# Quantising w1 and w2 with the contraction on the partitions: maxima from blocks on the rows, scales through memory, no transposes

## The reference, cut to what matters

```python
def nf4_quant_dequant(w):                      # blocks of 64 along each row of w
    flat = w.reshape(-1, 64)
    absmax = jnp.max(jnp.abs(flat), axis=1, keepdims=True)
    normalized = flat / jnp.where(absmax == 0, 1.0, absmax)
    idx = jnp.searchsorted((NF4_CODE[:-1] + NF4_CODE[1:]) * 0.5, normalized)
    return (NF4_CODE[idx] * absmax).reshape(shape)

dq1, dq2, dq3 = (nf4_quant_dequant(w) for w in (w1, w2, w3))   # (1376,512), (1376,512), (512,1376)
h = silu(x @ dq1.T) * (x @ dq2.T)
return layernorm(x + h @ dq3.T)
```

## Time and profile before

| | |
|---|---|
| median of 3 runs (lowest, highest) | 429.75 us (429.55, 430.0) |
| time of the profiled execution | 429.79 us |
| its span, first to last instruction | 428.0 us |
| granted TensorE clock, mean over the span | 0.994 |
| busy: PE, PEld, DVE | 418.1, 343.0, 309.3 us |
| busy: ACT, POOL | 260.4, 274.5 us |
| DMA | 26.51 MB in 10876 packets |

### The profile page before, as it was taken

The page is one execution under the profiler, slowest core; times in us unless marked ns, Lnnn a source line. Parts: engine busy times, 40 slices in busy tenths (PEclk is TensorE's granted clock), DMA queues, the critical chain, the costliest instruction groups (busy, mean ns, idle before and its releaser), DMA issues.

```text
span 428.0 us, 5616 instructions
## 1 busy us (share of the span) xinstructions
PE 418.1 (98%) x1908; PEld 343.0 (80%) x1908; DVE 309.3 (72%) x390; ACT 260.4 (61%) x345; POOL 274.5 (64%) x219
## 2 busy tenths in 40 slices
PE   8999999999999999999999999999999999999992
PEld 7888888888878887888878888888888878888881
DVE  4539979788779979955568999998998884215025
ACT  5576766585586565548746786788667763332612
POOL 0079898798695699238953667699866853344330
PEclk9999999999999999999999999999999999999997
DMA  7994110100114432020060000000000000000202
GB/s 269 398 356 149 51 38 25 27 25 26 25 49 130 137 123 74 0 100 1 0 265 1 2 0 2 0 2 1 1 2 0 2 0 0 2 2 2 98 0 99
DMA packets 10876, 26.51 MB, mean 62 GB/s; under 512 B 1472, under 2 KB 1728, under 8 KB 10336
## 3 DMA queue, kind: packets, MB, share of 16 engines
q1 hardware_dynamic: 10848, 26.16, 17.9%
HBM read 24.06 MB, written 2.10 MB: 61 GB/s over the span
## 4 chain that ended last, share of the span: by engine, by line
PE 84%; POOL 8%; issue 5%; DVE 2%; ACT 0%; POOLq 0%
PE PS L1145 27%; PE PS L1147 27%; PE PS L1146 26%; POOL l_lo L1100 4%; PE PS L1259 2%; PE PS L1277 1%; POOL level L1070 1%; PE PS L1270 1%; POOL w_lo L1089 1%; POOL x_lo L1089 1%; DVE stats L876 0%; POOL Q L1061 0%; DVE R L871 0%; PE PS L1245 0%; ACT R L644 0%
## 5 line engine op out<-in xcount | busy, mean ns | idle before, releaser
L1070 POOL TENSOR_SCALAR level<-side 128x1024 f32<-128x1024 int8 (+2 forms) x119 | 130.0, 1093 | 25.9 <-ACT side L558 15.8
L801 DVE TENSOR_TENSOR PS<-PS,level 128x1024 f32<-128x1024 f32 (+2 forms) x102 | 121.8, 1194 | 24.1 <-POOL level L1070 19.8
L1145 PE MATMUL PS<-x_hi,w_hi 128*128 128x512 f32 (+1 forms) x352 | 138.4, 393 | 0.0
L1147 PE MATMUL PS<-x_hi,w_lo 128*128 128x512 f32 (+1 forms) x352 | 137.2, 390 | 0.0
L1146 PE MATMUL PS<-x_lo,w_hi 128*128 128x512 f32 (+1 forms) x352 | 137.1, 389 | 0.0
L558 ACT ACTIVATE side<-Q 128x1024 int8<-128x1024 f32 (+1 forms) x77 | 77.6, 1050 | 13.3 <-DVE PS L797 7.2
L1100 POOL TENSOR_TENSOR l_lo<-h,l_hi 128x512 fp32r<-128x512 f32 (+1 forms) x42 | 56.3, 1348 | 42.3 <-ACT l_hi L558 41.6
L1147 PEld LDWEIGHTS PS<-x_hi,w_lo 128*128 128x128 f32 (+1 forms) x352 | 65.2, 185 | 14.7
L1145 PEld LDWEIGHTS PS<-x_hi,w_hi 128*128 128x128 f32 (+1 forms) x352 | 65.3, 185 | 14.4 <-issue 0.3
L1146 PEld LDWEIGHTS PS<-x_lo,w_hi 128*128 128x128 f32 (+1 forms) x352 | 65.3, 185 | 14.3
L1145 PE MATMUL PS<-x_hi,l_hi 128*128 128x512 f32 x144 | 56.8, 395 | 0.6 <-POOL l_lo L1100 0.6
(11 more groups left out here) (77 smaller groups left out, 509.0 us busy)
## 6 DMA issues: line engine op xcount, KB each, us to landing
Q<-w SPq DMA_DIRECT2D x20, 256.0 KB, 9.8
raw<-w_in SPq DMA_DIRECT2D x9, 512.0 KB, 9.1
raw<-w_out SPq DMA_DIRECT2D x14, 256.0 KB, 2.6
raw<-w SPq DMA_DIRECT2D x2, 1376.0 KB, 7.8
R<-xN SPq DMA_DIRECT2D x2, 1024.0 KB, 5.2
out<-R SPq DMA_DIRECT2D x8, 256.0 KB, 2.1
raw<-w_fuse SPq DMA_DIRECT2D x7, 256.0 KB, 2.7
h<-xT SPq DMA_DIRECT2D x3, 512.0 KB, 6.6
```

What stands on the lines that cost most here:

```text
L801: v.tensor_tensor(total, total, level_of(s), ALU.add).then_inc(s_add, 1)
L1070: g.tensor_scalar(level_of(s), side_of(s), LIMITS[k][1], LIMITS[k][0], ALU.min, ALU.max).then_inc(s_level, 1)
L1145: t_.matmul(dst, a_hi, b_hi, start=start, stop=False)
L1147: return t_.matmul(dst, a_lo, b_hi, start=False, stop=stop)
```

## The change

For units 1 to 10 (`turned`) the maxima and the codes are computed on two layouts of the same numbers. The host passes w1 and w2 in two forms: `w12`, where a unit's blocks of 64 lie so that the 128 partitions get the blocks in order (`natural`, read only for the maxima), and `w12T`, with the contraction on the partitions, in the layout that the products read. DVE takes maxima and reciprocals from the first; SP writes both to a scratch tensor `scr` in memory (`to_memory`) and reads them back broadcast, each over the 64 partitions of its block, to full width (`from_memory`: four DMAs for a unit, in contiguous runs of up to 128 numbers). POOL then multiplies the turned unit by the full-width reciprocals (`rcp_wide`), DVE the sum by the full-width maxima (`amax_wide`). The result needs no transpose: `split_nf4` and `lo_nf4` read Q. Unit 0 is done as before.

These moves stand in SP's list between the loads of the weights, in the order `MOVES`, as many at each place as a new list `SHARE["sync"]` says. Their buffers: the last two units of Q while those are not in use, `raw`'s columns 4096 to 5119 (so `raw` has four slots instead of five for the weights, and splits are done three jobs ahead instead of four), and for unit 10 `raw` and two slots of `l_hi`. Scales are made 12 steps ahead (7 for unit 10). w3's first half is loaded when unit 10 is normalised, its second when unit 9 is dequantised. All SHARE lists are new, and two splits on ACT stand ahead of the last `scale_and_shift` of layer 1.

```diff
-SCALES_AHEAD, NORMALISE_AHEAD = 5, 3
+TURNED_AHEAD, LAST_AHEAD, SCALES_AHEAD, NORMALISE_AHEAD = 12, 7, 5, 3
...
+MOVES = [(1, "scales"), (2, "natural")]
+for u_ in range(1, C2):
+    MOVES.append((u_, "rcp"))
+    if u_ + 1 < C2:
+        MOVES.append((u_ + 1, "turned"))
+        if u_ + 2 == C2:
+            MOVES.append((u_ + 1, "natural"))
+        MOVES.append((u_ + 1, "scales"))
+        if u_ + 2 < C2 - 1:
+            MOVES.append((u_ + 2, "natural"))
+    MOVES.append((u_, "amax"))
+MOVES += [(C2 - 1, "w3 first"), (C2 - 1, "w3 second")]
...
-RAW_SLOTS = 5
-W_AHEAD = 4
+RAW_SLOTS = 4
+W_AHEAD = 3
...
 SHARE = {
+    "sync": [
+        0, 2, 1, 1, 5, 2, 3, 2, 5, 3, 4, 3, 2, 3, 0, 0, 0, 0, 0, 0, 0, 0, 0, 2, 0, 0, 0, 2, 0, 3, 0, 7, 0],
...
+            def to_memory(u):
+                n = unit_blocks(u)
+                sp.wait_ge(s_prep, scaled(u))
+                if u >= 3:
+
+                    sp.wait_ge(s_at, 32 * (u - 2))
+                for k, t in enumerate((amax, rcp)):
+                    sp.dma_start(scr[u % 2, k, 0:P * n].rearrange("(p n) -> p n", n=n), t[:, u % t.shape[1], 0:n]).then_inc(s_scr, 16)
+
+            def from_memory(u, k, to, done):
+                p = chunk_rows(u)
+                sp.wait_ge(s_scr, 32 * u)
+                blocks = scr[u % 2, k, 0:2 * DC * 2 * p].rearrange("(q r f) -> r q f", r=2, f=p)
+                for r in range(2):
+                    sp.dma_start(to[r * BLOCK:(r + 1) * BLOCK, 0:2 * DC * p].rearrange("p (q f) -> p q f", f=p),
+                                 blocks[r:r + 1].broadcast_to([BLOCK, 2 * DC, p])).then_inc(done, 16)
...
+            def rcp_back(u):
+                if u >= 2:
+                    sp.wait_ge(s_nrm, normalised(u - 1))
+                if u == C2 - 1:
+                    wait_split(sp, len(JOBS) - 1)
+                    wait_split(sp, VECTOR_LOW[-1])
+                from_memory(u, 1, rcp_wide(u), s_rc)
+
+            def amax_back(u):
+                if u >= 2:
+                    sp.wait_ge(s_dq, quantised(u - 1))
+                if u == C2 - 1:
+
+                    sp.wait_ge(s_tile, TT)
+                from_memory(u, 0, amax_wide(u), s_at)
+
+            def load_natural(u):
+
+                sp.wait_ge(s_prep, scaled(u - 1))
+                if u == C2 - 1:
+                    wait_split(sp, len(JOBS) - 1)
+                    wait_split(sp, VECTOR_LOW[-1])
+                load_unit(u)
...
             for j in range(RAW_SLOTS, len(JOBS)):
                 if j == JOB[1, AGAIN[0]]:
+                    beside()
                     load_residual(0)
+                beside()
                 load_job(j)
+            beside()
             load_residual(1)
-
-            wait_split(sp, len(JOBS) - 1)
-            wait_split(sp, VECTOR_LOW[-1])
-            for q in range(2):
-                sp.dma_start(w3_tile(q), w3[q * P:(q + 1) * P, :]).then_inc(s_w3[q], 16)
+            beside()
...
             def split_nf4(f):
                 beside()
-                m = rows(f, F2)
-                act.wait_ge(s_tr, f + 1)
+                n = 2 * DC * rows(f, F2)
+                if f == 0:
+                    act.wait_ge(s_tr, 1)
+                else:
+                    act.wait_ge(s_dq, quantised(f))
                 wait_nf4_slot(act, f)
-                copy(in_slot(w_hi, f, 2 * DC * m).rearrange("p (c m) -> p c m", m=m),
-                     PS[:, NF4_BANK:NF4_BANK + 2, :].rearrange("p b (c m) -> p (b c) m", m=P)[:, :, 0:m]
-                     ).then_inc(s_whi4, 1)
+                copy(in_slot(w_hi, f, n), nf4_chunk(f)).then_inc(s_whi4, 1)
...
             root_of_variance(1, 2)
-            scale_and_shift(1, 2)
             split_x(TILES)
             split_x(TILES + 1)
+            scale_and_shift(1, 2)
...
+                    if turned(u):
+                        dve.wait_ge(s_at, 32 * u)
+                        v.tensor_tensor(unit_read(u), total, amax_wide(u)[:, 0:unit_width(u)],
+                                        ALU.mult).then_inc(s_dq, 1)
+                        return
...
             def lo_nf4(f):
                 beside()
-                m = rows(f, F2)
-                n = 2 * DC * m
+                n = 2 * DC * rows(f, F2)
                 dve.wait_ge(s_whi4, f + 1)
                 wait_nf4_slot(dve, f)
-                v.tensor_tensor(in_slot(w_lo, f, n).rearrange("p (c m) -> p c m", m=m),
-                                PS[:, NF4_BANK:NF4_BANK + 2, :].rearrange("p b (c m) -> p (b c) m", m=P)[:, :, 0:m],
-                                in_slot(w_hi, f, n).bitcast(F32).rearrange("p (c m) -> p c m", m=m),
+                v.tensor_tensor(in_slot(w_lo, f, n), nf4_chunk(f), in_slot(w_hi, f, n).bitcast(F32),
                                 ALU.subtract).then_inc(s_wlo4, 1)
...
+                    if turned(u):
+                        pool.wait_ge(s_qT[u], 16)
+                        pool.wait_ge(s_rc, 32 * u)
+                        g.tensor_tensor(unit_read(u), unit_read(u), rcp_wide(u)[:, 0:unit_width(u)],
+                                        ALU.mult).then_inc(s_nrm, 1)
+                        continue
...
-                if x in (11, 13):
-                    transpose_nf4((x - 11) // 2)
+                if x == 11:
+                    transpose_first()
...
-                elif i == 2:
-                    transpose_nf4(2)
-                elif half == 1 and f + 2 < C2:
-                    transpose_nf4(f + 2)
```

More of the change, by code:

```diff
@@ L115, with turned, chunk_rows, unit_blocks @@
 UNITS = C2 + 2 * W3_PARTS
+def turned(u):
+    return 0 < u < C2
+def chunk_rows(u):
+    return min(P, F2 - u * P)
 def unit_rows(u):
-    return min(P, F2 - u * P) if u < C2 else P
+    return P
+def unit_blocks(u):
+    return chunk_rows(u) // 8 if turned(u) else UW // BLOCK
 def w3_place(u):
@@ L142, with steps_ahead, scales_due, normalise_due @@
 STEPS = [(u, k) for u in range(UNITS) for k in range(NB)]
-SCALES_AHEAD, NORMALISE_AHEAD = 5, 3
-def units_ahead(s, ahead):
-    return [u for u in range(UNITS) if max(0, NB * u - ahead) == s]
+TURNED_AHEAD, LAST_AHEAD, SCALES_AHEAD, NORMALISE_AHEAD = 12, 7, 5, 3
+def steps_ahead(u):
+    return SCALES_AHEAD if not turned(u) else TURNED_AHEAD if u < C2 - 1 else LAST_AHEAD
+def scales_due(s):
+    return [u for u in range(UNITS) if max(0, NB * u - steps_ahead(u)) == s]
+def normalise_due(s):
+    return [u for u in range(UNITS) if max(0, NB * u - NORMALISE_AHEAD) == s]
+MOVES = [(1, "scales"), (2, "natural")]
[10 more added lines that the diff above has]
+MOVES += [(C2 - 1, "w3 first"), (C2 - 1, "w3 second")]
 def adds(s):
@@ L328, in build @@
         s_q = [sem(f"s_q{i}") for i in range(C2)]
+        s_qT = [sem(f"s_qT{i}") for i in range(C2)]
+        s_scr, s_rc, s_at = sem("s_scr"), sem("s_rc"), sem("s_at")
         s_w3 = [sem(f"s_w3_{q}") for q in range(2)]
@@ new lines, in load_natural, with move @@
+            def load_natural(u):
+                sp.wait_ge(s_prep, scaled(u - 1))
+                if u == C2 - 1:
+                    wait_split(sp, len(JOBS) - 1)
+                    wait_split(sp, VECTOR_LOW[-1])
+                load_unit(u)
+            def move(i):
+                u, what = MOVES[i]
+                if what == "scales":
+                    to_memory(u)
+                elif what == "rcp":
+                    rcp_back(u)
+                elif what == "natural":
+                    load_natural(u)
+                elif what == "amax":
+                    amax_back(u)
+                elif what == "turned":
+                    if u >= C2 - 2:
+                        sp.wait_ge(s_nrm, normalised(u - 1))
+                    load_turned(u)
+                elif what == "w3 first":
+                    sp.wait_ge(s_nrm, normalised(u))
+                    load_w3(0)
+                else:
+                    sp.wait_ge(s_dq, quantised(u - 1))
+                    load_w3(1)
@@ L513, in load_residual, with beside @@
+            turn, done = iter(SHARE["sync"]), [0]
+            def beside():
+                for _ in range(next(turn)):
+                    move(done[0])
+                    done[0] += 1
             def load_residual(a):
@@ L1057, in clamp_step @@
             def clamp_step(s):
-                for u in units_ahead(s, NORMALISE_AHEAD):
+                for u in normalise_due(s):
+                    if turned(u):
+                        pool.wait_ge(s_qT[u], 16)
[3 more added lines that the diff above has]
+                        continue
                     pool.wait_ge(s_prep, scaled(u))
@@ L1353, in chunks_in, with blocks_of @@
         return np.ascontiguousarray(np.concatenate(parts, axis=1))
+    def blocks_of(*ws):
+        parts = [np.concatenate([w[0:P] for w in ws], axis=1)]
+        for u in range(1, C2):
+            m = chunk_rows(u)
+            both = np.stack([w[u * P:u * P + m].reshape(m, D // BLOCK, BLOCK) for w in ws])
```

(5 more changed lines are left out.)

68 lines of the change are left out of this document (42 added, 26 removed), and 20 rows, old and new, of the table SHARE.

## The result

The changed kernel takes **446.14 us** in the median of 6 runs (444.28 to 449.43), the kernel before 429.74 (6 runs, 429.55 to 430.08): ratio 1.0383, 95% interval 1.0362 to 1.0404. It is slower by 16.4 us where I forecast 6.9 us faster; neither the range (420.6 to 427.6) nor a rival (D's 433 the highest) held it. The profiled execution was the fastest of the six, 444.28 us; its span is 442.5 us against 428.0.

What follows compares the result with a forecast made beforehand. PE's list of work was taken as the bound, busy 418.1 of 428.0 us. From 429.79 us, less 8.5 for removed transposes, plus a 1.5 stall at unit 10, came 422.8 us; range 420.6 to 427.6.

Steps and rivals of the forecast that it cites:

- D: Rival: short 512 B packets fill the DMA queue from the in-projection on, unit 10 12 us late, 433 us; chance 0.06.
- Hidden: SP's queue: about 8.4 us of added queue time per unit every 18 us, weight loads behind the moves, costing PE nothing.
- what PE does not have to do is won: Whole kernel: PE, busy 418.1 of 428.0 us, sets the time, so work removed is gained if nobody makes it wait.
- Nothing lost: Quantiser steps moved earlier: no loss in 234 to 355 us (bounds 0 and 3) or 13 to 217 us (0 to 2).
- 26 us free: First layer's in-projection: DVE's spare time, set against six more steps there, 8 us.
- Removed, 8.5 us: Ten of eleven blocks of eight transposes leave PE: units 1 to 9 give 7.83 us, unit 10 0.66.
- (a): lo_nf4 on DVE reads codes from Q instead of PSUM: 0.4 us more each, 0 to 1.1, 4 us in ten.
- (b): POOL's normalising product takes a full-width reciprocal: at most +0.75 us each, about 6 us over the first 220 us.
- (c) and (d): DVE's dequantising product keeps one PSUM input, unchanged at 1224 ns; ACT splits from SBUF at the same width, nothing added.
- Packets, 45 ns each: Broadcast reads in 512 B runs on the DMA queue: 45 ns per packet, thus 2.9 us for 1024 packets.
- Unit 10's trip: Unit 10's scales through memory, 212.4 to 229.0 us, delay ACT's scaling of tiles 4 and 5: PE stalls 1.5 us, bounds none and 7.
- Rival C: DVE and POOL hold each other, last dequantising 2 to 4 us after PE asks before w3's transposes: 424.5 to 427; chance 0.20.

Runs made afterwards that it cites:

- e1_swap: Changed kernel with SP's read-back of the next unit's reciprocals put ahead of this unit's maxima, nothing else: 432.84 us, ratio 1.0054 to the kernel before.
- e8_half_before: Kernel before with DVE's additions for units 1 to 10 over half of each row: 428.81 us, ratio 0.9978.
- e11_free_psum: e5_free with DVE's low-half subtraction for units 1 to 10 reading its first operand from PSUM (stale data): 428.30 us, ratio 0.9963.
- e5_free: Kernel before without the transposes of units 1 to 10, splits reading Q untransposed; old SHARE lists and five slots kept: 432.62 us, ratio 1.0056.
- e12_half_free_all: e5_free with DVE's additions halved in all units but the first, w3's included: 424.51 us, ratio 0.9871 to the kernel before.
- e6_narrow: e3_noback with POOL's normalising product taking reciprocals spread per block again instead of a full-width second input: 430.19 us, ratio 0.9998.
- e4_slots: Kernel before with four slots in raw instead of five and splits three jobs ahead: 432.39 us, ratio 1.0051.
- e3_noback: Changed kernel with scales neither written to memory nor read back, wide products taking the unit itself as second operand: 430.37 us, ratio 1.0001.
- e2_contig: Changed kernel with broadcast reads of units 1 to 9 taken from 4 KB rows of other data, order and waits kept: 442.2 us (one run).

## Why the prediction was wrong

**The step that failed first** is the last word under "Added: DMAs on SP's queue": *Hidden*. I summed what the queue has to carry and asked whether it fits into time; I did not write down for what SP waits ahead of each entry. In MOVES "amax" of u stands ahead of "rcp" of u + 1 and waits for the dequantising of u - 1. That one order is 14.1 of the 23.4 us between my forecast and the result (e1_swap). I had asked what is queued behind the waiting instruction for ACT at unit 10, and not for SP.

**The second** is the start of the sum, *time is PE's list of work ... what PE does not have to do is won*, and *Nothing lost* under "Moved earlier". The kernel before is bound by PE (e8_half_before: DVE relieved, 1 us). But the side engines are not far behind: take 8.5 us from PE and leave their lists, and 1.6 us are won with DVE's operand in PSUM (e11_free_psum); with it in SBUF, as the change has it, it is 2.6 us longer (e5_free). I had the room as 99 us of 113, from busy sums over 121 us. A busy sum does not hold the order: DVE's step waits for POOL's level, which waits for ACT's side, and h, which PE wants, stands behind it. Every microsecond that PE is earlier makes these lists late by one. Halving DVE's additions brings 8.0 us back (e5_free to e12_half_free_all); the remainder is idle time of PE, in which POOL seems to be next. Moving nine steps earlier helps layer 2's pairs (e1_swap: 102.11 of 103 us busy in 262 to 365), and PE loses 5.1 us in 131 to 190 instead (e1_swap). In the in-projection I had added 8 us to DVE and counted "26 us free" as if any of it could be used; in e1_swap it is 10.6 us more (102.3 busy of 118, before 91.7), and 50 to 80 us is full.

**The idle time costs more than its length.** I never priced the clock. After PE's waits of 3.9 us (changed kernel), 3.2 (e1_swap) and 2.9 (e5_free) a stretch of five microseconds stands at 0.50, 0.50 and 0.57. In the changed kernel the two stretches from 150 to 160 (0.50 and 0.85) lose 3.3 us, most of the 5.4 by which PE is busier than 409.6; in e5_free it is the clock of 0.93 over 300 to 350.

The other terms, one by one:
- *Removed, 8.5 us*: right as work of PE: 8.9 less busy in e12_half_free_all against e8_half_before.
- *(a), 0.4 each, 0 to 1.1*: 1.50 in the median against 1.22, the mean of the nine full ones 1.73: 0.5, up to 1.1 (2317 ns). Size right, consequence wrong: I held it hidden, and it costs 4.0 us where DVE is the one waited for (e11_free_psum), 1.3 to 3.2 of them by the clock. The rule that I weighed there (Trainium skill, SBUF — State Buffer, "Who interferes with whom") spoke against the edit and the trace bears it out in kind: from PSUM 1.21, from SBUF 1.82. It does not hold each for a whole instruction of POOL, though the worst pair comes near: POOL's product took 4.79 us where it mostly takes 2.41, and DVE's residual addition beside it 2.86, at least 0.67 elsewhere (the DMA engines were at 0.97 as well then, so this pair doesn't show the cause alone).
- *(b), at most +0.75*: 2415 ns in the median against 1906, so +0.5. No effect on the time that shows (e6_narrow).
- *(c) and (d), nothing*: right. DVE's dequantising product takes 1225 ns against 1224, ACT's high half 1059 in the mean from SBUF against 1027 from PSUM.
- *Fewer slots*: named, given no price; 2.2 us (e4_slots).
- *Packets, 45 ns each*: too high by a third. The queue's packets take 32.4% of 16 engines' 442.5 us in the changed kernel (34768 of them) and 21.4% of 16 x 428.4 in e3_noback (10768), which has the same loads and no trip: 827 us for 24000 packets, 34 ns. That is inside my 25 to 99, and rival D falls (e2_contig). The trip's reads of 256 KB landed after 5.3 us into Q and 4.3 into `raw`, near the 4.9 that I had for unit 10's.
- *Unit 10's trip, 16.6 us from the load of its blocks to the end of ACT's two steps* (212.4 to 229.0): it ran from 234.85 to 251.33, 16.5. The place was right too: PE waits there for ACT's scaling, 0.8 us where I said 1.5. Its first and last row in the chain:

```profile
234.85 3.25 DMA raw<-w
...
251.33 0.95 ACT R L793 x2
```

Rival C had half of the mechanism (DVE's list fills, PE waits for it, POOL and DVE hold each other) and placed it at the start of w3, one wait; it came at several places, where PE was early. The place that I watched closest was worked out right, and the cost lay in the periodic part, which I had passed over in a sentence. "Wrong in kind if the pairs of the first layer pause" was my own test, and it came true: 4.0 us in 13 to 131.

The 23.4 us then, by ratios: 14.1 the order of two waits; 2.3 the rest of the round trip (e1_swap to e3_noback); 7.0 what e3_noback still lacks. There PE waits mostly for the low halves that DVE and POOL make, and halving DVE's additions takes 7.1 us off e1_swap; some 2 of it may be the slots, if that price carries over (not tried there). How much of it is (a) within the new lists was not tried either: e11_free_psum has it in the old ones. Lists between the old and the new, which might divide the loss, stay open.

## What to carry to other kernels

Write an in-order queue down as pairs "waits for, then releases" and walk one period of it: an entry that waits for something late, put ahead of one that is ready, makes a loop that no sum of bytes or busy time shows. An engine at 98% is the bound only for the next microsecond; before counting on eight, take the instruction that it will ask for earlier (here h) and count what stands ahead of it in its producer's list, in the fullest 50 us and not in the whole stretch. And the cheapest test of such a gain is to leave the work out of the old kernel, with nothing else changed, before the machinery that replaces it is built: e5_free would have said that with these lists there was nothing to win.

## What the runs showed of the hardware

- A wait of PE can cost more than its length. PE's wait of 2.9 us in e5_free, to 311.38, is followed by a granted clock of 0.57 in 310 to 315 and 0.74 in 315 to 320, and by matmuls 0.43 us apart instead of 0.23. e1_swap's of 3.2 us is followed by 0.50 in 136 to 141, the changed kernel's of 3.9 by 0.50 in 150 to 155. In the profiled execution of e11_free_psum no wait between 13 and 420 us was longer than 2.1 us, and the clock stayed at full level.
- SP took about 0.6 us to issue one broadcast read in 512 B runs (0.61 and 0.64 in the median), and 0.53 to 0.57 for one of the same size in 4 KB rows (e2_contig), where a load of weights took 0.33 to 0.38: four broadcast reads are 2.5 us of SP's time a unit.
- A DVE subtraction of 128x1024 with both operands in SBUF took 1.82 us in the median (e5_free, POOL busy 74% of 220 to 340 us), 1.21 with one in PSUM (e11_free_psum).
- A POOL product of 128x1024 took 2.42 us with a second input of full width and 1.91 with 16 numbers a row spread over their blocks.
